# A three-layer field-interaction network: W2 loaded in another layout instead of being turned, and the start, the first group and the end arranged anew

## The reference

```
x_vec = x
for W, b in ((W0, b0), (W1, b1), (W2, b2)):      # W: 128 x (H * 64)
    z     = einsum('bhd,bfd->bhfd', x_vec, x)     # H = 64, then 128, 128
    x_vec = einsum('oc,bcd->bod', W, z.reshape(B, H * 64, 16)) + b
    outs.append(x_vec.sum(axis=2))                # over d
return concatenate(outs, axis=1)                  # 512 x 384
```

## Time and profile before

| | us |
|---|---|
| median of 3 runs (1091.85 to 1092.72) | 1092.18 |
| the profiled execution | 1091.6 |
| its span, first to last instruction | 1089.5 |
| TensorE busy (98% of the span) | 1064.6 |
| VectorE busy (81%) | 877.3 |
| GpSimd busy (79%) | 859.6 |
| ScalarE busy (65%) | 710.3 |

### The profile page before, as it was taken

The page is one execution under the profiler, slowest core; times in us unless marked ns, Lnnn a source line. Parts: engine busy times, 40 slices in busy tenths (PEclk is TensorE's granted clock), DMA queues, the critical chain, the costliest instruction groups (busy, mean ns, idle before and its releaser), DMA issues.

```text
span 1089.5 us, 18056 instructions
## 1 busy us (share of the span) xinstructions
PE 1064.6 (98%) x4783; PEld 803.5 (74%) x4783; DVE 877.3 (81%) x2673; ACT 710.3 (65%) x2447; POOL 859.6 (79%) x727
## 2 busy tenths in 40 slices
PE   5999999999999999999999999999999999999997
PEld 5777777777778777777778777777778877777676
DVE  5768989889874888989894798989886598888881
ACT  4666767676764767767673676777675576767770
POOL 2668997989884897989985799898987589898550
PEclk9999999999999999999999999999999999999998
DMA  7942423332322323323241232433332133320000
GB/s 275 245 92 81 101 71 71 96 76 78 66 70 58 76 78 69 85 57 97 66 87 40 56 97 66 88 84 69 94 79 59 47 69 97 76 79 28 1 23 8
DMA packets 108327, 85.88 MB, mean 79 GB/s; under 512 B 71040, under 2 KB 73824, under 8 KB 108096
## 3 DMA queue, kind: packets, MB, share of 16 engines
q1 hardware_dynamic: 106832, 78.17, 29.3%
q10 hardware_dynamic: 1392, 6.55, 1.9%
HBM read 14.75 MB, written 0.79 MB: 14 GB/s over the span
## 4 chain that ended last, share of the span: by engine, by line
PE 90%; DVE 3%; ACT 2%; DMA 2%; POOL 1%; issue 1%; ACTq 0%; SPq 0%; DVEq 0%; POOLq 0%
PE y L913 62%; PE l L934 9%; PE l L913 8%; PE xt L1021 5%; PE l2p L1033 4%; DVE acc L769 2%; DMA gram<-in_L_rec_W_dram 1%; PE l2p L1010 1%; ACT y L662 1%; DMA z<-xg 1%; ACT prod L673 1%; POOL z L453 1%; DVE gram L851 1%; PE l L922 0%; POOL pacc L463 0%
## 5 line engine op out<-in xcount | busy, mean ns | idle before, releaser
L769 DVE SCALAR_TENSOR_TENSOR acc<-y,x0t,acc 128x128 f32<-128x128 f32 x2048 | 559.8, 341 | 101.8 <-PE y L913 99.1
L673 ACT ACTIVATE prod<-y,x0t 128x128 f32<-128x128 f32 x1280 | 365.8, 379 | 157.4 <-PE y L913 148.6
L913 PE MATMUL y<-w1h,x1h 128*128 128x512 f32 x1024 | 464.6, 454 | 2.2 <-DVE acc L769 1.4
L913 PE MATMUL y<-w1h,x1l 128*128 128x512 f32 x1024 | 402.1, 393 | 0.0
L913 PE MATMUL y<-w1l,x1h 128*128 128x512 f32 x1024 | 400.6, 391 | 0.0
L453 POOL TENSOR_TENSOR z<-z,xg 128x512 f32<-128x512 f32 (+2 forms) x272 | 352.5, 1300 | 32.8 <-DMA z<-xg 32.8
L463 POOL TENSOR_TENSOR pacc<-pacc,prod 128x512 f32<-128x512 f32 x192 | 268.0, 1396 | 79.7 <-ACT prod L673 78.3
L913 PEld LDWEIGHTS y<-w1h,x1h 128*128 128x128 f32 x1024 | 193.2, 189 | 96.8 <-issue 26.5
L662 ACT ACTIVATE y<-y,x0t 128x128 f32<-128x128 f32 x512 | 142.6, 342 | 157.4 <-PE y L913 157.2
L913 PEld LDWEIGHTS y<-w1l,x1h 128*128 128x128 f32 x1024 | 192.8, 188 | 59.3 <-issue 28.8
L913 PEld LDWEIGHTS y<-w1h,x1l 128*128 128x128 f32 x1024 | 192.1, 188 | 43.0
(11 more groups left out here) (85 smaller groups left out, 673.0 us busy)
## 6 DMA issues: line engine op xcount, KB each, us to landing
z<-xg SPq DMA_DIRECT2D x480, 128.0 KB, 2.4
w2t<-in_L_rec_W_dram SPq DMA_DIRECT2D x8, 512.0 KB, 7.1
gram<-in_L_rec_W_dram ACTq DMA_DIRECT2D x8, 512.0 KB, 7.4
xg<-in_r_input_dram SPq DMA_DIRECT2D x30, 128.0 KB, 3.8
z<-xg SPq DMA_DIRECT2D x32, 96.0 KB, 5.9
z<-xg SPq DMA_DIRECT2D x15, 192.0 KB
gram<-in_L_rec_W_dram ACTq DMA_DIRECT2D x1, 2048.0 KB, 9.2
out_dram<-z SPq DMA_DIRECT2D x4, 192.0 KB, 1.9
```

The lines of the kernel that those rows point to most:

```text
L673: last = nc.scalar.activation(prod[:, h % HSLOTS, k, :], y[c % YB][:, k * O:(k + 1) * O], ACT.Copy, scale=x0t[:, j, f:f + 1])
L769: ins = nc.vector.scalar_tensor_tensor(out=to, in0=of, scalar=x0t[:, j, f:f + 1], in1=b1r[:] if m == 0 else to, op0=ALU.mult, op1=ALU.add)
L913: ins = nc.tensor.matmul(to, stationary, moving, start=(first and k == 0), stop=(last and k == 2))
```

## The change

- `w2t` has the shape [h, o, f] instead of [h, f, o]. W2 is loaded into it directly during group 1, in eight DMAs on ScalarE's queue whose rows are 64 values (256 B) long. `turn_w2` and `w2_out` are gone. The quarter's stationary operand is `w2t[:, :, f]`, 128 values 64 elements apart.
- W1's eight load DMAs move from the SP queue to ScalarE's queue, behind a wait for x.
- In the first group GpSimd's products are dealt to other gaps, layer 0 of group 1 starts two steps later, and layer 2 of the first tile is no longer put off by two steps.
- W0's pair sums are cut into other pieces with fewer elements in all. Six transposes of the identity come after the first turn of W0, and W0's last round is turned before a batch of layer 0.
- At the end: 24 transposes of the identity while TensorE waits for the last tile; a reduction becomes two adds; the copies of the last layer-2 product are split between ScalarE and VectorE; the last quarter takes gram as the stationary and W2 as the moving operand, so its result has batch rows on the partitions, gets b2 added by VectorE and is stored in a DMA of its own; the rows of layers 0 and 1 are turned in the middle of it.

The diff without its context lines and without new names for memory and semaphores (`w0stage` is the new name of `w2raw`):

```diff
+LAST_CLOCK_KEEPERS = 24
-W2_AT = 14
+CLOCK_KEEPERS = 6
-W2_LOAD_AT = [k * 3 // 2 for k in range(W_PARTS)]
+W2_LOAD_AT = [4 + 7 * k for k in range(W_PARTS)]
-LATER_PRODUCTS = (6, (0, 1, 4, 3, 3))
+LATER_PRODUCTS = (6, (3, 0, 5, 3, 0))
-AHEAD_FIRST_AT = [24 + t * 31 // (ZT - 1) for t in range(ZT)]
+AHEAD_FIRST_AT = [26 + t * 29 // (ZT - 1) for t in range(ZT)]
-PARTED_FIRST_AT = [{AHEAD_FIRST_AT[t] - k: t for t in PARTED} for k in (5, 4)]
+PARTED_FIRST_AT = [{AHEAD_FIRST_AT[t] - k: t for t in PARTED} for k in (5, 3)]
-PRODUCTS_FIRST_AT = ((0, 0, 0, 0, 0), (2, 1, 1, 1, 2), (2, 1, 2, 1, 2), (2, 0, 0, 0, 0))
+PRODUCTS_FIRST_AT = ((0, 0, 0, 0, 0), (0, 3, 1, 0, 1), (3, 3, 1, 1, 4), (0, 0, 0, 0, 0))
...
-def layer2_at(n, j):
-    return LAYER2_AT + 2 if n == 0 and j == 1 else LAYER2_AT
...
-        w2t = sb("w2t", [P, F, O])
+        w2t = sb("w2t", [P, O, F])
...
+        b2r = sb("b2r", [P, O])
...
-                sp.wait_ge(xturned_made, 1)
-                for k in range(W_PARTS):
-                    part = slice(k * F * O // W_PARTS, (k + 1) * F * O // W_PARTS)
-                    sp.dma_start(w1raw[:, part], w1[:, part]).then_inc(w1_loaded if k < W1_FIRST else w1_rest_loaded, 16)
...
-            for r in range(B // P):
+            sp.dma_start(b2r[:], b2.rearrange("(a o) -> a o", a=1).to_broadcast((P, O))).then_inc(b2r_loaded, 16)
+            for r in range(B // P - 1):
-            sp.wait_ge(stored, 16 * (B // P))
+            last_rows, ahead = slice(B - P, B), slice(0, (L - 1) * O)
+            sp.wait_ge(outs_made, B // P)
+            sp.dma_start(out[last_rows, ahead], outs[:, B // P - 1, ahead]).then_inc(stored, 16)
+            sp.wait_ge(last_rows_made, 1)
+            sp.dma_start(out[last_rows, (L - 1) * O:L * O], outs[:, B // P - 1, (L - 1) * O:L * O]).then_inc(stored, 16)
+            sp.wait_ge(stored, 16 * (B // P + 1))
...
+            act.wait_ge(x_loaded, 32)
+            for k in range(W_PARTS):
+                part = slice(k * F * O // W_PARTS, (k + 1) * F * O // W_PARTS)
+                act.dma_start(w1raw[:, part], w1[:, part]).then_inc(w1_loaded if k < W1_FIRST else w1_rest_loaded, 16)
...
-            def w2_out(c):
-                act.wait_ge(w2_turned, c + 1)
-                nc.scalar.copy(w2t[:, CF * c:CF * c + CF, :], l2p[:, c % 2, :].rearrange("p (f o) -> p f o", o=O)) \
-                    .then_inc(w2_kept, 1)
...
-                    act.wait_ge(w0l_made, W0_STEPS - 1)
-                part = slice(k * F * O // W_PARTS, (k + 1) * F * O // W_PARTS)
-                act.dma_start(w2raw[:, part], w2[:, part]).then_inc(w2_loaded, 16)
+                    act.wait_ge(w1_turned, CHUNKS)
+                part = slice(k * O // W_PARTS, (k + 1) * O // W_PARTS)
+                act.dma_start(w2t[:, part, :], w2[part, :].rearrange("o (h f) -> h o f", f=F)).then_inc(w2_loaded, 16)
...
-                    if kind == "first" and e in W2_LOAD_AT:
+                    if n == 1 and e in W2_LOAD_AT:
...
-                    if kind == "first" and W2_AT <= e - 1 < W2_AT + CHUNKS:
-                        w2_out(e - 1 - W2_AT)
-                    if c == layer2_at(n, j) + 1 and (kind != "first" or j > 0):
+                    if c == LAYER2_AT + 1 and (kind != "first" or j > 0):
...
-            layer2_out(GROUPS * TILES - 1, (QG * TILES - 1) * TILE_B)
-            quarter_out(QUARTERS)
-            row_out(B // P - 1)
+            act.wait_ge(l2p_made, layer2_ready(GROUPS * TILES - 1))
+            nc.scalar.copy(gram[:, :, QB - TILE_B:QB - HALF_B], l2p[:, 0, 0:GRAM].rearrange("p (b f) -> p f b", f=F))
+            nc.scalar.copy(sums1[:, B - TILE_B:B - HALF_B], l2p[:, 0, GRAM:GRAM + HALF_B]).then_inc(l2p_used, 1)
+            act.wait_ge(turned, B // P)
+            nc.scalar.copy(outs[:, B // P - 1, 0:(L - 1) * O], l0[:, 0:(L - 1) * O]).then_inc(outs_made, 1)
...
-                add_pairs(at(w0pair, F * s0 + half, [F, n], [1, half]),
-                          at(w0raw, (F + 1) * half + F * s0, [F, n], [F + 1, half]),
-                          at(w0raw, (F + 1) * half + s0, [1, n], [F + 1, half]))
-                add_pairs(at(w0pair, F + (F - 1) * s0, [F - 1, n], [1, half - 1]),
-                          at(w0raw, F - s0, [-1, n], [F + 1, half - 1]),
-                          at(w2raw, F * F - F * s0, [-F, n], [F + 1, half - 1]))
-                add_pairs(at(w0pair, F * s0, [F, n], [1, half]),
-                          at(w0raw, F * s0, [F, n], [F + 1, half]),
-                          at(w0raw, s0, [1, n], [F + 1, half]))
+                near, edge = F - s0, n - 1
+                add_pairs(at(w0pair, F * s0, [F, n], [1, near]),
+                          at(w0stage, s0, [1, n], [F + 1, near]),
+                          at(w0stage, F * s0, [F, n], [F + 1, near]))
+                if r > 0:
+                    add_pairs(at(w0pair, F * s0 + near, [F, n], [1, s0]),
+                              at(w0stage, (F + 1) * near - near, [1, n], [F + 1, s0]),
+                              at(w0stage, (F + 1) * near - F * near, [F, n], [F + 1, s0]))
+                add_pairs(at(w0pair, F + (F - 1) * s0, [F - 1, n], [1, edge]),
+                          at(w0stage, F * F - F * s0, [-F, n], [F + 1, edge]),
+                          at(w0stage, F - s0, [-1, n], [F + 1, edge]))
+                if r == 0:
+                    add_pairs(at(w0pair, 0, [F, n], [1, edge]),
+                              at(w0stage, 0, [1, n], [F + 1, edge]),
+                              at(w0stage, 0, [F, n], [F + 1, edge]))
...
-            nc.vector.tensor_reduce(x2[:, slot], acc[:, slot].rearrange("p k o -> p o k"), AX.X,
-                                    ALU.add).then_inc(x2_made, 1)
+            nc.vector.tensor_tensor(acc[:, slot, 0:2], acc[:, slot, 0:2], acc[:, slot, 2:4], ALU.add).then_inc(acc_step, 1)
+            dve.wait_ge(acc_step, tile_added(tile) + 2)
+            nc.vector.tensor_tensor(x2[:, slot], acc[:, slot, 0], acc[:, slot, 1], ALU.add).then_inc(x2_made, 1)
+            dve.wait_ge(b2r_loaded, 16)
+            nc.vector.tensor_scalar(b2r[:], b2r[:], float(D), None, ALU.mult).then_inc(b2r_made, 1)
+            dve.wait_ge(l2p_made, layer2_ready(tile))
+            nc.vector.tensor_copy(gram[:, :, QB - HALF_B:QB],
+                                  l2p[:, 1, 0:GRAM].rearrange("p (b f) -> p f b", f=F)).then_inc(gram_half_made, 1)
+            nc.vector.tensor_copy(sums1[:, B - HALF_B:B], l2p[:, 1, GRAM:GRAM + HALF_B]).then_inc(gram_half_made, 1)
+            dve.wait_ge(b2r_made, 1)
+            dve.wait_ge(l2_made, QUARTERS)
+            nc.vector.tensor_tensor(outs[:, B // P - 1, (L - 1) * O:L * O], l2, b2r[:], ALU.add).then_inc(last_rows_made, 1)
...
-            def turn_w2(c):
-                if c >= 2:
-                    pe.wait_ge(w2_kept, c - 1)
-                else:
-                    pe.wait_ge(w1l_made, CHUNKS)
-                for k in range(CF):
-                    last = nc.tensor.transpose(l2p[:, c % 2, k * O:(k + 1) * O],
-                                               w2raw.rearrange("o (h f) -> o f h", f=F)[:, CF * c + k, :], ident[:])
-                last.then_inc(w2_turned, 1)
+                    if q == 1:
+                        pe.wait_ge(w2_loaded, 16 * W_PARTS)
-                    last = nc.tensor.matmul(l2, w2t[:, f, :], gram[:, f, :], start=(f == 0), stop=(f == F - 1))
+                    last = nc.tensor.matmul(l2, w2t[:, :, f], gram[:, f, :], start=(f == 0), stop=(f == F - 1))
...
+            for _ in range(CLOCK_KEEPERS):
+                nc.tensor.transpose(y[W0_STEPS - 2][:, 0:P], ident[:], ident[:])
+            turn_w0(W0_STEPS - 2)
-            turn_w0(W0_STEPS - 2)
...
-                    if kind == "first" and W2_AT <= e < W2_AT + CHUNKS:
-                        if e == W2_AT:
-                            pe.wait_ge(w2_loaded, 16 * W_PARTS)
-                        turn_w2(e - W2_AT)
-                    if c == layer2_at(n, j) and (kind != "first" or j > 0):
-                        if kind == "first" and j == 1:
-                            pe.wait_ge(w2_kept, CHUNKS)
+                    if c == LAYER2_AT and (kind != "first" or j > 0):
...
+            pe.wait_ge(outs_made, B // P - 1)
+            for _ in range(LAST_CLOCK_KEEPERS):
+                nc.tensor.transpose(l0[:, (L - 1) * O:L * O], ident[:], ident[:])
-            for part in range(QUARTER_PARTS):
-                quarter(QUARTERS, part, 2 * GROUPS)
-            turn_row(B // P - 1)
+            pe.wait_ge(x0t_made, 2 * GROUPS)
+            pe.wait_ge(l2p_used, GROUPS * TILES + 1)
+            pe.wait_ge(gram_half_made, 1)
+            for f in range(F):
+                if f == F // 2:
+                    pe.wait_ge(gram_half_made, 2)
+                    for k in range(L - 1):
+                        last = nc.tensor.transpose(l0[:, k * O:(k + 1) * O], sums[:, k, B - P:B], ident[:])
+                    last.then_inc(turned, 1)
```

(18 more changed lines are left out.)

## The result

The changed kernel takes 1128.17 us (median of 4 runs, 1127.42 to 1128.22), the kernel before 1092.45 beside it (1091.85 to 1093.49): a ratio of 1.032, interval 1.031 to 1.034. It is slower; 1088.7 was forecast, with a range up to 1097. The profiled execution took 1128.13, with a span of 1126.4.

The account below looks back on a forecast made before the run. TensorE, busy 98% of the span and most of the chain, was taken as the bound. Terms of -15.0 and +11.5 for the quarters made -3.5 from 1091.6: 1088.1, as a median 1088.7 us, range 1074 to 1097.

Parts of the forecast that it names:

- The price of a strided weight load: Three inner layer-2 quarters: 256-B step adds 0.030 us to each of 3 x 128 loads, 11.5 lost; bounds 0 and 42.
- rival (b): Quarters: strided loads cost in full, 0.110 us on each of 384, +42.2, giving 1119.4; chance 0.16.
- The moving operand: Last quarter, W2 as strided moving operand: no loss taken; bounds 0 and 14 us.
- The first group: Without W2's turns and load, first tile gains 2.5 us, the rest 8.5, with GpSimd's products 2 late for last layer-0 steps.
- Rival (c): ScalarE's W1 issues and GpSimd's third tile take back half of start and first-group gain, 12.2 to 6.1: 1094.8; chance 0.08.
- The start: Before the first chunk: shorter W0 sums and earlier W1 loads against ScalarE's queue, gain 1.2 us; bounds 2.5 lost, 2.5 gained.
- W2's new load: Group 1: eight short-row issues on ScalarE's queue delay chunk multiplies, cost 0.7 us; bounds 0 and 3.
- The end: After the last chunk: adds, layer-2 product, copies, last quarter and store together 3.5 us less, if the 24 transposes keep the clock.
- rival (d): End: the 24 transposes do nothing for the clock, so 0.5 and 1.6 us stay: 1090.8; chance 0.06.
- The sum without the two strided terms: Whole kernel: first group -8.5 and -2.5, start -1.2, W2 load +0.7, end -3.5, together -15.0 us.

Follow-up runs that it names:

- the bench: Changed kernel with layer 2's quarters turned into test cases of sixteen matmuls (product or transpose, steps, partitions, columns); 1123.16 us, one run.
- the kernel in parts: Changed kernel with W2 loaded in eight parts during groups two and three and copied by ScalarE into contiguous runs; reference's result; 1077.12 us, ratio 0.985.
- The step alone: Kernel before the change, with only the stationary operand of all four quarters read at the 256-B step; 1142.46 us, one run.
- the kernel without the step: Changed kernel with the layer-2 operand read as contiguous values, so layer 2 is not the reference's; 1075.8 us, one run.
- the two bench kernels: Changed kernel with inner quarters at varied operand steps, 1123.96 us, and with the quarters as test cases of products and transposes, 1123.16 us; one run each.

## Why the prediction was wrong

**The price of a strided weight load** is the step that failed, in "The quarters: the price that decides". I took 0.030 from W1's turns, between bounds of 0 and 0.110; it is 0.108, all but the upper bound, and rival (b) to within its term (38.8 for 42.2, the difference being the 24 first loads of a part, and 0.002 on each of the rest). The rows I leaned on were of another kind of instruction. The turns at 256 B and the loads at 64 B are both transposes; the bench shows a transpose at 0.149 and 0.112 where a product takes 0.220 and 0.218.

That the upper bound came out right is luck. I had it from W2's turns, whose loads take 252 ns against 142. They are transposes too, and W1's turns, from which I took 0.141 as the pitch, have loads just as long:

```profile
L968 PEld LDWEIGHTS l2p<-ident,w2t x64: 221/253/268, 23.2 to 54.4; 128*128 128x128 f32 x64
```

So the 110 ns were no second price, but the 0.030 measured another way. The bench shows the same: with the step, the load of a transpose takes 120 ns more (first line; the second is contiguous) and its pitch grows by 0.040, while the load of a product takes 121 ns more (313 for 192) and its pitch grows by 0.108.

```profile
L1063 PEld LDWEIGHTS xt<-ident,w2t x8: 223/260/268, 314.4 to 315.5; 128*128 128x128 f32 x8
L1063 PEld LDWEIGHTS xt<-ident,w2t x8: 139/140/143, 317.1 to 318.0; 128*128 128x128 f32 x8
```

I had set against (b) that part of a load hides behind the matmul before it. Of a transpose's increase two thirds don't show in the pitch, of a product's hardly any; why they differ is open.

**The moving operand** was taken at 0, bounds 0 and 14. It is 13.8 (28.5, against 14.7 from 1059.41 in the kernel in parts, without the step), at its upper bound. The ground for 0, a value each 0.87 ns "what the 64-B loads got", was again the transposes. The Trainium skill's rule of lines (SBUF — State Buffer, Specifications), which I cited beside the sum and left without weight, would have put both terms at a loss.

**The first group** came out right in size: 2.8 for 2.5 in the first tile, 8.7 for 8.5 behind it, 50.69 for the 50.9 foretold. The cause that I gave for what is left there is not shown. GpSimd is busy nearly all of the third tile, 19.68 of its 19.84:

```profile
72.18:92.02 19.84, 19.05 (x75) 13.03 (x74) 15.06 (x42) 11.49 (x38) 19.68 (x16) 1.00 0.40 110
```

But TensorE idles only 0.79 there, and its two waits end with VectorE, one with the adding of a scaled chunk and one with the split of a layer-0 product:

```profile
75.70 0.50 PE L928 MATMUL y<-w1h,x1h 128*128 128x512 f32 x1 [0.44 <-DVE acc L753]
...
80.64 0.50 PE L928 MATMUL l<-zh,w0h 128*128 128x512 f32 x1 [0.35 <-DVE zl L717]
```

In the fourth tile, where late products of GpSimd's should have shown last, TensorE is busy for all of the 14.74. Rival (c) found no place.

**The start** gained 0.9 for 1.2, a loose number: the kernels with this same start began their first chunk between 25.01 and 25.59, and the kernel of "The step alone", whose start is that of the kernel before, at 28.23 for 26.17. The end of the first group is firmer: 106.0 to 107.5 in the seven kernels that share start and first group, or differ only in the dealing, against 119.2 and 119.7. ScalarE's queue did what the argument against it feared, without harm that shows: eight issues take 4.50 from 4.28, its table load begins at 8.88, 0.5 later than before. **W2's new load** cost 0.3 for 0.7, in a group where the DMA share is 0.68.

**The end** is right in all but the quarter: without the step it is 3.6 shorter, 3.5 was forecast. The keepers do hold the clock, so rival (d) falls: 24 transposes alone made the difference between 0.50 and 1.00 and 2.4 us. That speaks against the rule of the Trainium skill (TensorE: Matmul & The Clock Gate, Part 4: PE-mode transpose) that transposes don't count as busy in the same way, and here the measurement decides.

The sum without the two strided terms was -15.0; the kernel without the step measured -16.6 beside the kernel before. The range failed because the case with the upper bound had 0.16 and was left out; even that case, 1119.4, is 8.8 short, since it left the moving operand at 0.

## What to carry to other kernels

A layout that saves a transposition is paid for by whoever reads it: with at most one value per 16 bytes, on either operand, fp32 products here stood about twice as far apart (0.218 to 0.268 for 0.112, at 160 B 0.320), and 512 such instructions cost 52.4 us, where the first group, rid of W2's turns and load, gave 11.5. Price an operand from rows of the same kind of instruction (a product's load by a product's, a transpose's by a transpose's), and by the pitch, not by how long a load takes: 120 ns more on a load came to 0.040 of pitch in a transpose and to 0.108 in a product. Where there is no such row, the range has to hold the upper bound. If the turned layout is wanted, make the turn once on an engine with time to spare, in small parts, where the DMA engines are not busy: in parts it cost some 1.7 beside the load alone, with all loads in the first tile 6.4 there.

## What the runs showed of the hardware

- The pitch of an fp32 product with a 256-B step is 0.220 at a granted clock of 0.50 (0.215 to 0.220) and of 1.00 alike.
- A product with a step of 160 B on its weights takes 0.320, in two kernels; 12 and 44 values take 0.268 and 0.267. No reason was found.
- A transpose with a 64-B or 160-B step costs hardly more than a contiguous one (0.112 and 0.111 for 0.109), with 256 B 0.149.
- The granted clock fell to 0.50 in the last quarter of the kernel after (0.51 over 1096.5 to 1100.0), with TensorE at work in every moment of it, and in the two bench kernels with the same last quarter (0.50 over 1091.9 to 1095.3, 0.51 over 1091.6 to 1095.1); with contiguous operands and the same keepers it stayed at 1.00 there.
- A ScalarE copy of 128x512 fp32 from SBUF to SBUF takes 1.18 us with a step on either side; a contiguous cast takes 0.63. The copies into gram, which read PSUM with 64 values between neighbours, take only 0.61 (line 570 of the kernel in parts).
